# The rows of the first eight quads are made on chip in the setup, h is copied by two engines, and only GpSimd waits for the h table

## What is computed

```python
h_s = s @ lin1_ws * a * _inv(S_IN)                       # a: one number per node
h_v = jnp.einsum('nci,cd->ndi', v, lin1_wv) * a[:, :, None] * _inv(V_IN)
w = silu(edge_scalars @ fc_w1 * _inv(R)) @ fc_w2 * _inv(FC_HID)
es, ev = h_s[edge_src], h_v[edge_src]                    # one row of h for each edge
# products of w, es, ev and edge_attr for each edge, then
agg = segment_sum(mid, edge_dst, num_segments=n) * inv_nn
# lin2 on agg, plus sc on x, silu and gates
x = layernorm(x + gated)
```

## Time and profile before

| | |
|---|---|
| runs, median of 3 | 4014.98 us (4014.94 to 4015.94) |
| the profiled execution, its span | 4805.3 us |
| TensorE busy | 3953.4 us, 82% of the span |
| GpSimd busy | 2967.8 us, 62% |
| VectorE busy | 2421.9 us, 50% |
| ScalarE busy | 1987.8 us, 41% |
| first gather of h rows | 74.72 us |

### The profile page before, as it was taken

How to read it: one execution, slowest core, us unless ns; L and a number is a source line. 1 busy time by engine, 2 the same in 40 slices (tenths; PEclk the granted TensorE clock), 3 DMA queues, 4 the chain that set the end, 5 groups by cost and what they waited for, 6 DMA issues and landing times.

```text
span 4805.3 us, 64016 instructions
## 1 busy us (share of the span) xinstructions
PE 3953.4 (82%) x18658; PEld 1603.5 (33%) x18658; DVE 2421.9 (50%) x7622; ACT 1987.8 (41%) x5178; POOL 2967.8 (62%) x3160
## 2 busy tenths in 40 slices
PE   8778888888888888888888888888888888888887
PEld 5233333333333333333333333333333333333333
DVE  5455545555454544555555445555545545454544
ACT  3344444444444444344444344444444434444444
POOL 3666666666666666666666666666666666666664
PEclk9999999999999999999999989999999999999999
DMA  6443434343434343334343334343434333333333
GB/s 216 146 106 102 106 102 106 102 107 102 108 99 108 102 106 97 105 102 106 103 107 101 104 99 105 102 106 103 107 103 106 102 105 103 105 103 104 103 103 87
DMA packets 366207, 515.47 MB, mean 107 GB/s; under 512 B 66498, under 2 KB 245578, under 8 KB 365486
## 3 DMA queue, kind: packets, MB, share of 16 engines
q0 software_dynamic: 150768, 256.60, 22.7%
q10 hardware_dynamic: 164378, 180.74, 12.1%
q1 hardware_dynamic: 50724, 74.13, 5.1%
HBM read 431.15 MB, written 80.06 MB: 106 GB/s over the span
## 4 chain that ended last, share of the span: by engine, by line
another core or an unknown queue 35%; ACT 21%; PE 20%; issue 14%; ACTq 8%; SPq 0%; DMA 0%; DVE 0%; DVEq 0%
ACT aggsb L759 13%; ACTq L778 6%; PE pst_e L1061 6%; PE psg L1074 5%; PE psg L1072 5%; ACT tsum L783 3%; PE psw L1053 3%; ACTq L766 2%; ACT L804 1%; ACT hid L749 1%; PE psx L1097 1%; PE psx L1045 1%; ACT vec_s L800 0%; ACT L749 0%
## 5 line engine op out<-in xcount | busy, mean ns | idle before, releaser
L710 POOL DMA_INDIRECT rows<-h_table,src_cols x3125 | 2953.5, 945 | 1799.9 <-issue 894.8
L557 DVE TENSOR_TENSOR prod<-psw,rows 128x384 f32<-128x384 f32 (+2 forms) x3128 | 1210.1, 449 | 1680.8 <-remote 1264.3
L1072 PE MATMUL psg<-tsum,shifts 128*64 128x320 f32 x3126 | 1101.8, 478 | 653.3 <-ACT tsum L783 462.6
L1053 PE MATMUL psw<-fc,hid 128*128 128x448 f32 x3128 | 1424.0, 579 | 7.7 <-issue 1.7
L759 ACT ACTIVATE aggsb<-psg 32x160 f32<-32x160 f32 x3128 | 917.0, 293 | 927.2 <-remote 744.2
L1074 PE MATMUL psg<-tsum,shifts 128*64 128x288 f32 x3126 | 1009.2, 449 | 0.0
L1053 PEld LDWEIGHTS psw<-fc,hid 128*128 128x128 f32 x3128 | 549.0, 196 | 949.6 <-issue 840.1
L1061 PE MATMUL pst_e<-prod,sel 128*32 128x448 f32 x6256 | 811.9, 593 | 2.4 <-issue 2.4
L1072 PEld LDWEIGHTS psg<-tsum,shifts 128*64 128x64 f32 x3126 | 385.9, 144 | 1122.2 <-ACT tsum L783 774.3
L783 ACT ACTIVATE tsum<-pst_e 128x448 f32<-128x448 f32 x782 | 424.8, 543 | 499.0 <-remote 369.4
L1045 PE MATMUL psx<-es,fc 128*128 128x512 f32 x782 | 415.7, 613 | 175.5 <-ACT turned L788 120.5
(11 more groups left out here) (151 smaller groups left out, 1511.2 us busy)
## 6 DMA issues: line engine op xcount, KB each, us to landing
es<-in_esP ACTq DMA_DIRECT2D x391, 256.0 KB
agg_table<-aggsb ACTq DMA_DIRECT2D x782, 80.0 KB
rows<-h_table,src_cols POOLq DMA_INDIRECT x3125
nag<-agg_table SPq DMA_DIRECT2D x96, 320.0 KB
nxin<-in_xN SPq DMA_DIRECT2D x96, 208.0 KB
h_table<-hrow ACTq DMA_DIRECT2D x24, 320.0 KB, 4.2
out<-yn SPq DMA_DIRECT2D x95, 80.0 KB
xa<-in_xaT SPq DMA_DIRECT2D x24, 256.0 KB, 4.0
```

The lines of the kernel that those rows point to most:

```text
L557: return nc.vector.tensor_tensor(out, w_part, ev, ALU.mult)
L710: nc.gpsimd.indirect_dma_start(out=rows[:, u * QT + j, :], out_offset=None, in_=m.h, in_offset=bass.IndirectOffsetOnAxis(ap=m.src[:, t:t + ...
L1053: ins = nc.tensor.matmul(psw[b][:, 2 * c:2 * c + 2, 0:WN], hid[:, at:at + P], m.fc2[:].rearrange("p (t w) -> p t w", t=2)[:, :, 0:WN], sta ...
L1072: nc.tensor.matmul(psg[0:2 * W, 0:2 * AW].rearrange("p (s c) -> p s c", s=2), shifts[:, q % PRING, h, 0:2, :], low, start=(h == 0), stop=( ...
```

## The change

In the setup GpSimd gathers, for the 32 tiles of the first eight quads, rows of x with the node's number behind them (`xg`, 161 numbers a row, held in the room of `prod`). TensorE turns four tiles at a time (`turn`: four transposes of 128 features, and one of the last 32 features of all four tiles, which VectorE first joins in `xlast`). ScalarE copies the turned x to `xt`, VectorE its last part to `xzt`, and the same two halves of matmuls as for a chunk of nodes make the rows of h, which go into `rows` and never to HBM. So the setup has 33 units: 25 chunks ("h") and eight x units ("x"), in an order written out by hand (`XBEFORE`). In each unit ScalarE copies the first half, VectorE the second. VectorE's table work is cut into pieces, one for each unit. SP loads `dst` and `tbase` behind four chunks instead of eight, and four small tables of quad bases behind them; the fc weights are loaded by SP at its end. The buffers of the setup lie in the room of the later edge columns. SP no longer waits for the stores of h; GpSimd does, and ScalarE before it loads the edge columns of that room. In the edge block GpSimd starts with quad 8, each of quads 8 to 15 waiting until the quad that held its slot is summed; up to quad 47 it may run ahead, and from quad 48 (`LOOSE`) on the old wait holds.

The diff, cut to its core:

```diff
+LOOSE = 6 * RING
...
+AHEAD = RING
+XBEFORE = [6, 9, 11, 14, 16, 19, 21, 24]
+UNITS = [unit for c in range(HCHUNKS + 1) for unit in [("h", c)] + [("x", j) for j in range(AHEAD) if XBEFORE[j] == c]]
...
+        later = m.e4[:, E4_FIRST:TILES, :].rearrange("p t k -> p (t k)")
...
+        xa = later[:, 0:at_xz].rearrange("p (s n) -> p s n", s=SLOTS)
+        xz = later[:, at_xz:at_hrow].rearrange("p (s n) -> p s n", s=SLOTS)
+        hrow = later[:, at_hrow:at_hrow + SLOTS * CB * F].rearrange("p (s b f) -> p s b f", s=SLOTS, f=F)
+        flat = m.prod[:].rearrange("p r t w -> p (r t w)")
+        xg = flat[:, 0:AHEAD * QT * XW].rearrange("p (t f) -> p t f", f=XW)
...
-        n_w = 16 * (len(loads) + len(late))
+        n_w, n_fcw = 16 * len(loads), 16 * len(late)
...
+            def load_x(c, width):
+                if c >= SLOTS:
+                    sp.wait_ge(s_high, second_halves(unit_of("h", c - SLOTS)) + 1)
+                    sp.sem_inc(s_tick, 1)
+                sp.dma_start(xa[:, c % SLOTS, 0:width], io["xaT"][:, c * CB * P:c * CB * P + width]).then_inc(s_xin[c % SLOTS], 16)
+                sp.dma_start(xz[:, c % SLOTS, :], io["xzT"][:, c * P:c * P + P]).then_inc(s_xin[c % SLOTS], 16)
...
+            for c in range(1, 4):
+                load_x(c, CB * P)
             sp.dma_start(m.dst[:], io["dstT"]).then_inc(s_dst, 16)
             sp.dma_start(tbase[:], io["tile_base"].to_broadcast([P, TILES])).then_inc(s_dst, 16)
...
+            for j in range(QT):
+                sp.dma_start(qbase[W * j:W * j + W, :], io["quad_base"][j:j + 1, :].to_broadcast([W, QUADS])).then_inc(s_dst, 16)
+            for c in range(4, HCHUNKS):
+                load_x(c, CB * P)
+            load_x(HCHUNKS, rest)
...
-            for c in range(SLOTS):
-                sp.wait_ge(s_hout[c], 16 * (rounds + (2 if c == 0 else 0)))
...
+            sp.wait_ge(s_fc, 1)
+            sp.sem_inc(s_tick, 1)
+            for dst, src in late:
+                sp.dma_start(dst, src).then_inc(s_fcw, 16)
...
-            pool.wait_ge(s_fc, 1)
-            for dst, src in late:
-                pool.dma_start(dst, src).then_inc(s_w, 16)
-            pool.wait_ge(s_w, n_w)
+            pool.wait_ge(s_src, 16)
+            for t in range(AHEAD * QT):
+                nc.gpsimd.indirect_dma_start(
+                    out=xg[:, t, :], out_offset=None, in_=io["xg"],
+                    in_offset=bass.IndirectOffsetOnAxis(ap=m.src[:, t:t + 1], axis=0)).then_inc(s_xrow[t // QT], 16)
...
+            def high_half(n, kind, c):
...
+                dve.wait_ge(s_high, second_halves(n) + 1)
+                if kind == "h":
+                    out, scale = hrow[:, c % SLOTS, 2:CB, :], a_rows[:, CB * c + 2:CB * c + CB].unsqueeze(2)
+                else:
+                    out, scale = m.rows[:, QT * c + 2:QT * c + QT, :], xg[:, QT * c + 2:QT * c + QT, F:XW]
+                nc.vector.tensor_tensor(out, psh[n % 2][:, 1, 0:2 * F].rearrange("p (b f) -> p b f", f=F),
+                                        scale.to_broadcast([P, 2, F]), ALU.mult).then_inc(s_highcp, 1)
...
+                if n == 6:
+                    dve.wait_ge(s_dst, 32 + 16 * QT)
+                    then(local_nodes(0))
+                if n == 7:
+                    then(local_nodes(1))
...
+                if n == 10:
+                    reach()
+                if n == 11:
+                    extreme(0, m.local[:], ALU.max)
...
+                if 13 <= n < 17:
+                    lin2_weights(n - 13)
+                if n == 17:
+                    extreme(1, m.local[:], ALU.min)
+                if n == 18:
+                    extreme(2, m.off[:, :, 0], ALU.max)
+                if n == 19:
+                    extreme(3, m.off[:, :, 0], ALU.min)
...
+                if n == 21:
+                    extreme(5, delta[:], ALU.min)
...
+                if n + 1 < len(UNITS) and UNITS[n + 1][0] == "x":
+                    j = UNITS[n + 1][1]
+                    dve.wait_ge(s_xrow[j], 16 * QT)
+                    nc.vector.tensor_copy(xlast[:].rearrange("p (t c) -> p t c", c=V),
+                                          xg[:, QT * j:QT * j + QT, P:F]).then_inc(s_xlast, 1)
+                if kind == "x":
+                    dve.wait_ge(s_xps, c + 1)
+                    nc.vector.tensor_copy(xzt[:], pxz[:, 0:P]).then_inc(s_xzcp, 1)
+                if (kind, c) == ("h", HCHUNKS):
+                    continue
+                high_half(n, kind, c)
...
+            def turn(j):
+                pe.wait_ge(s_xrow[j], 16 * QT)
+                for t in range(QT):
+                    nc.tensor.matmul(pxt[:, P * t:P * t + P], xg[:, QT * j + t, 0:P], m.ident[:], start=True, stop=True,
+                                     is_transpose=True, skip_group_check=True)
+                pe.wait_ge(s_xlast, j + 1)
+                nc.tensor.matmul(pxz[:, 0:P], xlast[:], m.ident[:], start=True, stop=True,
+                                 is_transpose=True, skip_group_check=True).then_inc(s_xps, 1)
+            for n, (kind, c) in enumerate(UNITS):
+                if n + 1 < len(UNITS) and UNITS[n + 1][0] == "x":
+                    if UNITS[n + 1][1] == 0:
+                        pe.wait_ge(s_ident, 1)
+                    turn(UNITS[n + 1][1])
+                if kind == "h":
+                    keep_warm(256)
+                    pe.wait_ge(s_xin[c % SLOTS], 32 * (c // SLOTS + 1))
+                    left, last = xa[:, c % SLOTS, :], xz[:, c % SLOTS, :]
+                else:
+                    pe.wait_ge(s_xcp, c + 1)
+                    pe.wait_ge(s_xzcp, c + 1)
+                    left, last = xt[:], xzt[:]
...
+                if (kind, c) == ("h", HCHUNKS):
+                    half(n, 0, [P, LASTN], left, last).then_inc(s_low, 1)
+                else:
+                    half(n, 0, [P, P], left, last).then_inc(s_low, 1)
+                    if n >= 2:
+                        pe.wait_ge(s_highcp, second_halves(n - 1))
+                    half(n, 1, [P, P], left, last).then_inc(s_high, 1)
...
+            act.dma_start(m.src[:, 0:SRC_FIRST], io["srcT"][:, 0:SRC_FIRST]).then_inc(s_src, 16)
...
+            def low_half(n, kind, c):
...
+                act.wait_ge(s_low, n + 1)
+                for b in range(2):
...
+                    ins = nc.scalar.activation(out, psh[n % 2][r, 0, F * b:F * b + F], ACT.Copy, scale=scale)
+                ins.then_inc(s_lowcp, 1)
...
+            def store(c):
...
+                    act.wait_ge(s_highcp, second_halves(n) + 1)
+                    act.dma_start(m.h[c * (CB * P):(c + 1) * (CB * P), :].rearrange("(p b) f -> p b f", b=CB),
+                                  hrow[:, c % SLOTS, :, :]).then_inc(s_hout[c % SLOTS], 16)
...
+            for n, (kind, c) in enumerate(UNITS):
+                if kind == "x":
+                    act.wait_ge(s_xps, c + 1)
+                    nc.scalar.activation(xt[:], pxt[:], ACT.Copy).then_inc(s_xcp, 1)
+                low_half(n, kind, c)
+                if n and UNITS[n - 1][0] == "h":
+                    store(UNITS[n - 1][1])
+            if UNITS[-1][0] == "h":
+                store(UNITS[-1][1])
...
+            for c in range(len(m.h_stored)):
+                pool.wait_ge(m.h_stored[c], m.h_stores[c])
...
+            def freed(q):
+                if q < 2 * RING:
+                    return q - RING + 1
+                if q % GROUP:
+                    return 0
+                return q - RING + GROUP if q < LOOSE else q - 2
...
-                for q in range(QUADS):
+                for q in range(AHEAD, QUADS):
                     for j in range(QT if q < QUADS - 1 else LAST_REAL):
-                        gather(q, j, max(0, q - 2) if j == 0 and q % GROUP == 0 and q >= GROUP else 0)
+                        gather(q, j, freed(q) if j == 0 else 0)
...
+                if q == 0:
+                    for c in range(len(m.h_stored)):
+                        act.wait_ge(m.h_stored[c], m.h_stores[c])
...
-                dve.wait_ge(rows_loaded[u], 16 * (QT * I + tiles))
+                if loaded:
+                    dve.wait_ge(rows_loaded[u], 16 * (QT * (I - 1) + tiles))
```

More of the change, by code:

```diff
@@ L55 @@
 CB = 4
+SLOTS = 8
 AGG_ROWS = 99 * P
@@ L392, in _, with half @@
-            for c in range(SLOTS):
-                chunk(c, 0, [P] * CB, 32, c >= 2)
-                if c == 0:
+            def half(n, v, widths, left, last):
+                for b in range(2):
+                    out = psh[n % 2][0:widths[b], v, F * b:F * b + P]
+                    nc.tensor.matmul(out, left[:, (2 * v + b) * P:(2 * v + b) * P + widths[b]], lw1[:], start=True, stop=True)
+                r = slice(S * v, S * v + S)
+                both = psh[n % 2][:, v, 0:2 * F].rearrange("p (b f) -> p b f", f=F)[:, :, P:F]
+                return nc.tensor.matmul(both, last[r, :], lw1z[r, :], start=True, stop=True)
@@ L395, in _ @@
                     pe.wait_ge(s_row, 1)
-                    for n in range(2):
```

(12 more changed lines are left out.)

311 lines of the change are left out of this document (166 added, 145 removed).

## The result

The changed kernel takes 4079.7 us (median of four runs, 4076.3 to 4080.8) against 4015.0 us (4014.5 to 4015.9): ratio 1.0159, 95% interval 1.0145 to 1.0174. It is 64.8 us slower. The prediction said slower, 4045 us, and its range ended at 4064.

A forecast was written before the change was run, and what follows sets the result against it. GpSimd's gathers, 1.25 us each without pause, were taken as the bound. First gather 67.6 us later, 32 gathers removed (- 40.0), quad 48 + 2: + 29.6 us, so 4045 us, range 4014 to 4064.

The forecast's parts named there:

- the sign: Whole kernel: slower, with chance 0.80; same 0.12, faster 0.08.
- The bound: GpSimd's gathers set the kernel's time, issued without a pause at 1.25 us each.
- rivals that wanted another bound: Edge stage: sums, stores and copies set 5.0 us a quad, removed gathers gain nothing, 4072 us; chance 0.07.
- The clock: TensorE in setup: gaps of mostly 1 to 3 us may lower its granted clock; + 2 us, bounds 0 to 10.
- hand-shakes: Setup's x units: TensorE waits twice per unit on VectorE's copies; 13 us for eight, bounds 9 and 16.
- work of eight x units: TensorE in setup: two halves and five transposes, 2.75 us a unit, + 22 us.
- table work between them: VectorE in setup: table-check pieces stand in front of copies TensorE waits for; + 17 us, bounds 8 and 17.
- chunk 4 late: Setup loads: chunk 4 queues behind dst, tbase and qbase, so TensorE waits; + 7 us, bounds 0 and 9.
- quad 48: Edge stage: from there GpSimd may be only two quads ahead of the sums; + 2 us, 16 in a rival.
- Break-even: Setup's matmuls on TensorE would have to end at 101 us for no gain or loss.
- The parts costed at nothing: Setup: h copies on two engines, fc weights' loads moved to SP and added waits for the table, 0 us each.
- The profiled span of after: Profile of the changed kernel: 391 waiting gathers put its span some 790 us above its median, near 4835 us.

The follow-up runs named there:

- e1: The changed kernel with keep-warm matmuls filling TensorE's waits for chunk 4 and ahead of each x unit; 4042.9 us, ratio 1.0070 against the kernel before.
- e4: The changed kernel with the edits of e2 and e3 together; 4008.1 us, ratio 0.9986 against the kernel before.
- e2: The changed kernel with dst, tbase and qbase loaded behind eight chunks again and VectorE's table work three units later; 4074.6 us, ratio 1.0149.
- e3: The changed kernel with x_last gathered two units ahead, x_last_turned and x_turned copied one ahead, before table work and copies of halves; 4020.5 us, ratio 1.0016.
- e6: The changed kernel without x units, all 3125 gathers behind the setup; median 4032.5 us, runs 4024.6 to 4072.6, ratio 1.0038.
- e5: The changed kernel with e2's loads and table work moved to units where VectorE has no x-unit copy; 4051.2 us, ratio 1.0088.
- e9: The kernel of e6 with six keep-warm matmuls of 512 columns ahead of TensorE's wait for chunk 4; 4024.1 us, ratio 1.0023.
- e7: The kernel before, unchanged, profiled once more; 4012.9 us, profiled span 4011.1 us.
- e8: The kernel of e4 with six x units instead of eight, quads 6 and 7 gathered from the table; 4006.3 us, ratio 0.9984.
- e10: The kernel of e4 without the keep-warm matmul ahead of 23 of the 25 chunks; 4017.0 us, runs 4006.5 to 4028.1, ratio 1.0005.
- e11: The kernel of e4 with two keep-warm matmuls of 512 columns ahead of chunk 8 and two behind the last unit; 4017.6 us, ratio 0.9985.
- e12: The kernel of e8 with two keep-warm matmuls of 512 columns ahead of chunk 8 and two behind the last unit; 4013.7 us, ratio 0.9975.

## Why the prediction was right on the sign and wrong on the size

*The bound* held: 1.25 us a gather, 32 of them taken away. Of the rivals that wanted another bound nothing is left.

*The step that failed is the term "The clock", + 2 us, bounds 0 to 10.* It measured 37.3 us in the sum, 32.8 by filling the waits (e1), 38.8 by TensorE's busy time against e4. The prediction had seen 0.50 behind a gap of 4.39 us and allowed that shorter gaps might cost the same, but neither the 2 nor the 10 was worked out from anything. The runs showed a state that outlives its cause: once a wait has brought the clock down, at times one of 0.83 us (e2), the chunks take 4.39 instead of 2.44 us until it is back, and with an x unit at every third or fourth unit the next wait comes before, or soon after, that. A bound could have been worked out from the work behind the first wait: 21 chunks from chunk 4 on, 1.95 us each, are 41 us without the x units, if the clock never came back.

The sign needed no clock. In e1, where it is 1.00 throughout, the kernel is 29.4 us slower than before, against + 29.6 in the sum, which had 2 us for the clock. That this agrees to 0.2 us is in part luck, since the hand-shakes were put too high (below).

The Trainium skill (TensorE: Matmul & The Clock Gate, HAM oscillation — how this bites in real kernels) describes this pattern: short batches of matmuls with a wait for data between them, each paid for again at the lower level. The trace after agrees, 0.64 in the mean from 20 to 160 us, though most of its waits at x units, 0.55 to 4.15 us, are shorter than those in the page's example. The same page (What's actually happening) says that activity releases the throttle. e3 agrees, where the clock is back at 38.6 us; e6 does not, with 89.69 us busy of 89.70 at 0.50. There the measurement decides: gapless work does not guarantee the clock.

The other terms of the sum:

| step | forecast | measured |
|---|---|---|
| removed gathers | - 40.0 | - 40.0 |
| work of eight x units | + 22 | + 20.8 (e4: 2.60 us each) |
| hand-shakes | + 13 | about + 8 (last three x units: 0.83 + 0.83 + 1.25 us; e5: 9.3 for eight) |
| table work between them | + 17 | about + 16 (23.5 - 8) |
| chunk 4 late | + 7 | + 8.0, its load landing at 28.6 instead of 27 us; 5.7 without x gathers (e6), so the gathers slow it |
| later start of the chunks | 0 | + 1.4 |
| the clock | + 2 | + 37.3 |
| setup's end to the first h gather | 11.7 | 11.4 (171.7 - 160.3) |
| quad 48 | + 2 | + 3.1 |

The late chunk and the table work stalled TensorE where they were put. The hand-shakes did so only in part: where no table work is in the way, at the last three x units, TensorE does not wait for x_last at all, and its one wait is for ScalarE's copy x_turned, which the prediction had put beside the second wait. VectorE's timeline after, at the fourth x unit, shows the table work in front of the copy that TensorE's 2.99 us above waited for:

```profile
96.39 0.49 DVE L332 TENSOR_TENSOR e_cols<-psh,a_rows 128x320 f32<-128x320 f32 x1 [2.88 <-PE psh L498]
96.80 3.40 DVE L397 TENSOR_REDUCE ext<-dst_in_window 128x1 f32<-128x3128 f32 x1
100.12 0.22 DVE L470 COPY x_last<-prod 128x128 f32<-128x128 f32 x1
```

The stalls came to 31.5 us instead of 37. In e1, at full clock, waits and the fillers in them come to 127.5 - 69.3 - 20.8 = 37 us: at the lower clock TensorE's own work in front of a wait takes longer and covers more of it (for x_last at the fourth x unit TensorE waits 2.99 us in the profile after, and 3.6 us of fillers stand there in e1). *Break-even*, a setup that ends at 101 us, held: e3 ends at 103.7 and is 0.16% slower, e4 at 91.4 and is 0.14% faster. *The parts costed at nothing* cost nothing in the setup (e9). *The profiled span of after* was forecast near 4835 us and is 4074.4: the claim that 391 waiting gathers bring 790 us in any profile was wrong (e7).

Still open is why one wait brings the clock down and another of the same length does not (e4 and e8, 1.45 and 1.52 us), and why the clock comes back within 17 us in e3 and not within 90 in e6; the scatter of e6's and e10's runs, 48 and 22 us against 1.7 and 2.5 for the kernel before beside them, fits such a difference from one execution to the next, but was not traced run by run.

## What to carry to other kernels

When a change puts waits, however short, into a stretch in which TensorE has been gapless, take as the bound of the clock's price all the work behind the first wait at the lower clock, not the length of the wait: here 31.5 us of waits cost some 37 us more, and e6's single wait of 5.7 us cost 40.6 in its profile, but some 8 in the median. How much of the bound is paid could not be told beforehand. Order each consumer's engine so that the copy that TensorE waits for stands in front of work nobody waits for; this edit alone took back 58 of 65 us, while removing the largest single wait took back 4. And where a wait can't go, filler matmuls are worth trying: they gave 32.8 us of setup in e1 and 8 us of the median in e9. Where the clock hardly falls, as in e4, they gave nothing (e11).

## What the runs showed of the hardware that was not expected

The spacing of gathers is not quite a constant. It is 1.2499 to 1.2506 us in the mean in most profiled executions, from the first gather to the last without the longer waits for sums, and 1.2531 to 1.2533 us in those of e2, e9 and e11, just as evenly. Over 3100 gathers that is some 10 us, and it is also the distance between the medians of the kernel before in one set of runs (4023.6 us, with e11 and e12) and in the others (4013.4 to 4015.0); one run of before at 4023.7 us stands alone among twenty of 4012.6 to 4014.3. That these are the same thing was not traced. Differences of 0.2% between kernels can be read only against a kernel before that ran beside them.
